# Every product of the macaron block in plain fp32 instead of three fp32r parts

## The reference

```python
def _L0_ffn_ref(x, ...):
    shared = silu(x @ shared_gate.T) * (x @ shared_up.T) @ shared_down.T
    probs = sigmoid(x @ router_w.T + routing_bias)          # 8 experts
    scores, indices = top_k(probs, 2); scores /= sum(scores)
    g = silu(einsum('th,ehi->tei', xf, gate_w)); u = einsum('th,ehi->tei', xf, up_w)
    return shared + einsum('tei,eih,te->th', g * u, down_w, w)   # inner size 256
def _L0_attn_ref(x, ...):   # 16 heads of 8, linear attention over 256 tokens
    phi_q, phi_k = silu(q * s) + 1, silu(k * s) + 1
    return ((phi_q @ (phi_k.T @ v)) @ Wo.T + bo)
x = x + 0.5 * ffn(layernorm(x)); x = x + attn(layernorm(x)); x = x + 0.5 * ffn(layernorm(x))
```

## Time and profile before

| what | value |
|---|---|
| median of 3 runs | 795.73 us (795.63 to 799.72) |
| profiled execution | 798.22 us, of it 796.5 us span |
| PE busy | 682.1 us (86%) |
| DVE busy | 571.3 us (72%) |
| POOL busy | 533.0 us (67%) |
| ACT busy | 471.7 us (59%) |
| mean granted clock of TensorE | 0.921 |

### The profile page before, as it was taken

How to read it: one execution, slowest core, us unless ns; L and a number is a source line. 1 busy time by engine, 2 the same in 40 slices (tenths; PEclk the granted TensorE clock), 3 DMA queues, 4 the chain that set the end, 5 groups by cost and what they waited for, 6 DMA issues and landing times. The chain is left out here.

```text
span 796.5 us, 17786 instructions
## 1 busy us (share of the span) xinstructions
PE 682.1 (86%) x5133; PEld 639.2 (80%) x5133; DVE 571.3 (72%) x1886; ACT 471.7 (59%) x866; POOL 533.0 (67%) x564
## 2 busy tenths in 40 slices
PE   7574979772799999999789889999778999999990
PEld 6464869662799999999678788888677999999990
DVE  7778787771355787877688988899875555777672
ACT  5353453331467777786657666866425677777760
POOL 1457777777777777776166666777774577777672
PEclk9778788987899999999799999999979999999995
DMA  9312221141544555552122111111333535666545
GB/s 278 123 52 77 81 64 55 55 145 54 156 132 125 157 170 166 156 156 58 51 62 67 41 38 45 45 44 51 86 105 83 146 104 149 208 207 200 184 144 168
DMA packets 63337, 89.40 MB, mean 112 GB/s; under 512 B 13194, under 2 KB 43788, under 8 KB 63244
## 3 DMA queue, kind: packets, MB, share of 16 engines
q1 hardware_dynamic: 46348, 53.37, 23.4%
q0 software_dynamic: 16896, 34.90, 13.1%
HBM read 46.10 MB, written 42.12 MB: 111 GB/s over the span
## 5 line engine op out<-in xcount | busy, mean ns | idle before, releaser
L608 POOL DMA_INDIRECT x_rows<-send,send_to x256 | 248.5, 971 | 135.9 <-issue 71.6
L620 POOL DMA_INDIRECT y_rows<-send,y_to x272 | 264.2, 971 | 100.7 <-issue 73.7
L1637 DVE TENSOR_TENSOR h<-silu_g,u_bank 128x512 f32<-128x512 f32 x136 | 93.5, 687 | 114.3 <-ACT silu_g L758 107.8
L733 ACT ACTIVATE slot_gu<-w_gu 128x1024 fp32r x130 | 137.8, 1060 | 36.8 <-issue 36.7
L1013 PE MATMUL y_bank<-w_dn,h 128*128 x1088 | 143.7, 275 | 0.1
L1013 PEld LDWEIGHTS y_bank<-w_dn,h 128*128 128x128 f32 x1088 | 133.2, 192 | 0.3 <-issue 0.3
L855 PE MATMUL g_bank<-xT_hi,slot_gu 128*128 128x256 f32 x260 | 85.8, 330 | 9.9 <-DVE xT_lo L1628 9.2
L928 PEld LDWEIGHTS y_bank<-w_dn,h 128*128 128x128 f32 x512 | 69.2, 212 | 23.3 <-issue 20.6
L928 PE MATMUL y_bank<-w_dn,h 128*128 128x128 f32 x512 | 70.1, 296 | 19.0 <-DVE x L1234 19.0
L758 ACT ACTIVATE silu_g<-g_bank 128x512 f32<-128x512 f32 x136 | 78.8, 579 | 12.0 <-PE g_bank L857 11.5
L677 ACT ACTIVATE send<-x,shift,rstd 128x128 f32<-128x128 f32 x128 | 52.6, 482 | 37.7 <-DVE shift L1196 26.1
(11 more groups left out here) (270 smaller groups left out, 1626.0 us busy)
## 6 DMA issues: line engine op xcount, KB each, us to landing
send<-x_rows SPq DMA_DIRECT2D x130, 130.0 KB
y_pair<-y_rows SPq DMA_DIRECT2D x32, 512.0 KB
y_rows<-send,y_to POOLq DMA_INDIRECT x272
x<-x_in SPq DMA_DIRECT2D x16, 256.0 KB, 7.3
x_rows<-send,send_to POOLq DMA_INDIRECT x256
out<-x SPq DMA_DIRECT2D x16, 256.0 KB
w_raw<-w_experts SPq DMA_DIRECT2D x15, 256.0 KB, 3.1
x_rows<-pad SPq DMA_DIRECT2D x16, 130.0 KB, 2.4
```

The lines of the kernel that those rows point to most:

```text
L608: pool.indirect_dma_start(x_rows, bass.IndirectOffsetOnAxis(ap=send_to[b % SEND_TO_RING][:, w, k:k + 1], axis=0), send[ring_of(f, t)][:, w ...
L620: pool.indirect_dma_start(y_rows, bass.IndirectOffsetOnAxis(ap=y_to[k][:, j:j + 1], axis=0), y_out[f][k][:, j, :], None).then_inc(y_sent[k ...
L733: act.activation(slot_gu[n % 2][:].rearrange("p a n -> p (a n)"), w_gu[:, bass.ds(e, 1)].rearrange("p e a n -> p (e a n)").bitcast(F32), A ...
L1637: dve.tensor_tensor(h[par][0][:], silu_g[par][:], u_bank[par][:], ALU.mult).then_inc(slot_h_done, 1)
```

## The change

All high and low parts are gone, and each product is one plain fp32 matmul.

- `three`, `split_high`, `split_low`, `low`, `slot_low` and the router's split are removed. `gate_up`, `slot_gate_up`, `project`, `query` and `router` issue one matmul where there were three (router: two).
- The shared expert's weights are loaded straight to `w_gu`, those of the eight others by one DMA behind x. The loads through `w_raw` and their waits go.
- ACT's copy of a slot's weights is 512 columns instead of 1024. In a mixed slot ACT copies two experts' weights from `w_gu`, and `load_mixed_weights` and `mixed_gate_up` go.
- `route` has 25 steps instead of 26. `phi_k` and `v_sb` get buffers of their own.

```diff
+            sp.dma_start(w_gu[:, 0, :], w_experts[0, :, 0:2 * INNER]).then_inc(shared_loaded, 16)
...
+            sp.dma_start(w_gu[:, 1:, :], w_experts[1:, :, 0:2 * INNER].rearrange("e p n -> p e n")).then_inc(experts_loaded, 16)
...
-            for e in range(1, EXPERTS):
-                wait_count(sp, split_lo, 0 if e == 1 else split_expert(e - 2))
-                sp.dma_start(w_raw[e % 2][:], w_experts[e, :, 0:2 * INNER]).then_inc(w_loaded[e % 2], 16)
...
-                i = entry(s)
-                e = act.value_load(w_table[0:1, i:i + 1], min_val=1, max_val=ROUTED)
-                wait_count(act, slot_u_psum, n - 1)
-                act.activation(slot_gu[n % 2][:].rearrange("p a n -> p (a n)"),
-                               w_gu[:, bass.ds(e, 1)].rearrange("p e a n -> p (e a n)").bitcast(F32),
-                               ACT.Copy).then_inc(slot_gu_done, 1)
...
+                for j, i in enumerate(half_entries(s) if mixed(n) else (entry(s),)):
+                    e = act.value_load(w_table[0:1, i:i + 1], min_val=1, max_val=ROUTED)
+                    if j == 0:
+                        wait_count(act, slot_u_psum, n - 1)
+                    last = act.activation(slot_w[j][n % 2][:], w_gu[:, bass.ds(e, 1)].rearrange("p e n -> p (e n)"), ACT.Copy)
+                last.then_inc(slot_w_done, 1)
...
-                three(g_bank[k][:], (w[:, 0, g], w[:, 1, g]), xs)
-                three(u_bank[k][:], (w[:, 0, u], w[:, 1, u]), xs).then_inc(gu_psum, 1)
+                pe.matmul(g_bank[k][:], w[:, g], xT[par][:], start=True, stop=True)
+                pe.matmul(u_bank[k][:], w[:, u], xT[par][:], start=True, stop=True).then_inc(gu_psum, 1)
...
-                    pe.matmul(logits, xT_hi[t % XT_RING][:, s], router_parts[:], start=True, stop=False)
-                    last = pe.matmul(logits, xT_lo[t % XT_RING][:, s], router_parts[:], start=False, stop=True)
+                    last = pe.matmul(route_bank[:, (i + j) * ROUTED:(i + j + 1) * ROUTED], xT[t % XT_RING][:, s], router_w[:],
+                                     start=True, stop=True)
...
-                        last = three(bank_[:, c * ROWS:(c + 1) * ROWS], (w[:, 0, i], w[:, 1, i]), xs)
...
+                            last = pe.matmul(bank_[:, k:k + width],
+                                             w[par][:, base + c * P:base + (c + 1) * P],
+                                             xT[par][:, j * width:(j + 1) * width], start=True, stop=True)
...
-                dve.tensor_tensor(xT_lo[n % 2][:, 0:ROWS], slot_tr[n % 2][:, 0:ROWS],
-                                  xT_hi[n % 2][:, 0:ROWS].bitcast(F32), ALU.subtract).then_inc(slot_lo_done, 1)
```

More of the change, by code:

```diff
@@ L80 @@
 FIRST_STEPS, TABLE_STEPS = 19, 60
-TABLE_PIECES = {"last tile": (1, 8), "dispatched": (8, 22), "low": (22, 29), 0: (29, 35), 1: (35, 41)}
+TABLE_PIECES = {"last tile": (1, 8), "dispatched": (8, 22), "first slot": (22, 29), 0: (29, 35), 1: (35, 41)}
 TWO_BANKS_FROM = 2 * TILES - 2
@@ L134, in macaron @@
         x = sb("x", [P, tiles, TT])
-        w_raw = two("w_raw", [P, 2 * INNER])
-        w_gu = sb("w_gu", [P, EXPERTS, 2, 2 * INNER], F32R)
+        w_gu = sb("w_gu", [P, EXPERTS, 2 * INNER])
+        slot_w = [two(f"slot_w{j}_", [P, 2 * INNER]) for j in range(JS)]
         w_dn = sb("w_dn", [P, EXPERTS, HALVES, P])
[L139 to L146, removed]
+        w_attn_sb = sb("w_attn_sb", [P, 4 * P])
+        wo = w_attn_sb[:, 3 * P:4 * P]
+        router_w = sb("router_w", [P, ROUTED])
         bias_b = sb("bias_b", [P, ROUTED])
@@ L184, in macaron @@
         xn = two("xn", [P, SUB, P])
[L185 to L188, removed]
+        xT = ring(XT_RING, "xT", [P, TT])
+        attn_xT = two("attn_xT", [P, TT])
         send = ring(SEND_RING, "send", [P, PICKS, SUB, ROW])
@@ L381, in mixed @@
             return n % slots in MIXED_AT
[L383 to L387, removed]
         def entry(s):
@@ L1584, in dispatch @@
                     route(f, b, 0, MASK_STEP)
-                    if ahead:
-                        low((FFN, f, ahead[0]))
                     multiply_tile(f, ts[0])
@@ L1594, in dispatch @@
                         whole_table(f, 0, 1)
-                    if len(ahead) > 1:
-                        low((FFN, f, ahead[1]))
                     if b + 2 < len(BATCHES[f]) and NORM_OF[(FFN, f, BATCHES[f][b + 2][0])][1] == 0:
@@ L1656, in slot_stage @@
                         slot_results(f, s - 2)
-                    if s + 1 < slots:
-                        slot_low(f, s + 1)
                     if s == 0:
-                        table_piece(f, "low")
-                    if f == 0 and s == slots - 1:
-                        low((ATTN, 1, 0))
+                        table_piece(f, "first slot")
                     slot_multiply(f, s)
@@ L1682, in slot_stage @@
                 if f == 0:
-                    low((ATTN, 1, 1))
                     value(0, 0)
@@ L1751, in middle @@
                         mask_heads(i)
-                    if 0 <= i < tiles - 2:
-                        low((ATTN, 1, i + 2))
                     if 0 < i + 1 < tiles:
```

247 lines of the change are left out of this document (74 added, 173 removed).

## The result

The changed kernel takes 814.59 us (median of 4 runs, 812.58 to 815.06), the kernel before, run beside it, 797.3 (795.63 to 799.72). The ratio is 1.021, with a 95% interval of 1.017 to 1.025. Slower, as forecast, and inside the range, but by 17 us, where the forecast's own terms came to 35. The profiled execution took 814.64 us, 812.9 of it span.

The account below looks back on a forecast made before the run. PE was taken to bound the slot stages, POOL even with it, and DVE the attention turns. Terms 17.6 + 16.1 + 2 - 1 = +34.7 us on 798.2 gave 832.9, as median 830.4, forecast 830; range 811 to 846.

Parts of the forecast that it names:

- The price of a plain product: On PE, a plain record of 256 columns takes 0.217 us; a product takes 0.435 us against 0.352 for three fp32r parts.
- The first rival: On PE, wide plain records stream as fast as fp32r, a slot's products take 0.94 us; 774 us, chance 0.05.
- The slot stages: PE-bound full slots each take 0.34 us longer; +17.6 us in stage one, +16.1 us in stage two.
- POOL's stalls and its tail: Slower PE removes 2.5 us of full-ring stalls in stage one and 3.3 us behind stage two's last slots.
- The attention turns: PE takes over from DVE as bound, 12.8 us a turn over 15 turns; +2 us, bounds -18 and +16.
- Start and dispatch: Ahead of 55.25 us, DVE loses 4.6 us at most, longer products cost 2.5 to 5; -1 us, between -3 and +2.
- The eight slots ahead wait for rows and tables: Stage two's slots before slot 8 wait for rows and tables; no time change was counted for them.
- SP loses the loads of the mixed weights ... hidden: In SP's queue, the mixed slots' weight loads go away; claimed hidden, with no gain counted.
- nothing comes of it: In the slots, ACT's fewer copies and DVE's lost low part bring no gain, as both have a quarter of the stage free.
- The second rival: The attention turns give back all that DVE loses, -18 us instead of +2; 810 us, chance 0.13.
- the handover: The stretch from the last attention addition to slot 8 of stage two; forecast change 0 us.
- The third: PE-bound attention turns meet waits and low clock, 13.6 us a turn, and slots cost +0.37 us; 848 us, chance 0.17.

## Why the prediction came out as it did, step by step

**The price of a plain product** was right: 0.215 us for a record of 256 columns (0.217 forecast), 2.84 for a slot's period (2.86). The first rival, wide plain records as fast as fp32r, is refuted at its root; its bound was 0.176. That the number could be had from a single 0.21 in the earlier trace rows decided the case.

The Trainium skill (FP8 and Floating Point Precision, TensorE Precision Notes) with its four passes for fp32 stands: 4 x 256 columns at 2.4 GHz are an estimate of 0.427 us a product, and the trace has 0.43.

**The slot stages**: +15.9 and, with the tail, +15.7 us against 17.6 and 16.1. A slot costs 0.32 us more, not 0.34. POOL's stalls and its tail went as predicted: the end takes 3.1 us less (3.3).

**The attention turns**: -6.5 against +2. PE as the bound of the later turns was right, 12.6 us a turn (forecast 12.6 and 0.2 of waits), PE busy 129 of 130 us. That DVE had set them at 12.1 before is not what the trace shows: in turns 9 to 12 PE is busy 11.7 to 11.9 us and DVE 10.9 to 11.1, so PE was the fuller engine already, with a short wait for DVE's low part. The last eight took 94.4 us and take 98.7, +4.3, as the terms say.

The step that failed is the one that set all 15 turns at 12.8. The first seven took 93.9 us before, 13.4 on average, and take 83.2 (9.0 to 13.5). Of these 10.7 us, 8.1 lie in turns 1, 2, 4 and 7, which before ran at a mean clock of 0.77, 0.80, 0.81 and 0.88 and after at 1.00; the forecast had taken off 1.7 us for all 15 turns for the pauses and the clock. DVE's part is shown for the third to the sixth turn: idle work there costs 3.2 us. Why the clock stays full in after isn't known; in two kernels with the same work in the turns it fell again in the first two. So a mean over unlike turns hid a gain, and part of the gain is the clock.

**Start and dispatch**: +2.8 against -1. The forecast set longer products at half clock against DVE's relief and took the relief to win. The head got longer, and PE's products are on its chain: half of those of three tiles taken away brought the third batch forward. What share of the +2.8 is theirs isn't shown, and the +2.8 itself is known to 2 us only: in the seven kernels with the new head on chips like the first, slot 5's silu starts between 206.1 and 207.8, against 205.0.

**"The eight slots ahead wait for rows and tables"** was the larger miss: 12.0 of the 18 us by which the sum was off. The sentence was true and priced at nothing, as if rows and tables came when they came. They come by a chain that the change cut at two places. "SP loses the loads of the mixed weights ... hidden" was wrong: 4.3 us, shown by putting the loads back. And the slot's low part that DVE lost, 0.42 us, went into "nothing comes of it" as work of an engine with room, and not as what PE waits for: 4.8 us, shown by adding the wait, with its two idle subtracts, to after. Both stood in the trace of before, as 4.64 us of PE's idle time and as SP's queue. The sum of both, 9.1, leaves 2.9 of the 12.0, if they add. The kernel with three parts in the full slots alone, with SP's list of after, takes 54.6 us there, 7.7 above after and 4.3 below before; the 7.7 are the wait and 2.9 more, 0.8 of which stay with the first two slots plain (47.7). So most of the 2.9 goes with slots that are short while the table is late; how, wasn't taken apart.

**The second rival** (turns give back all that DVE loses, 810) named the right place and had a share of the truth: the measured 814.6 lies nearer to its 810 than to 830, but the turns gave 6.5 us, not 18, and the handover gave the rest. The third (848) is refuted: the clock stood at half for 89 us of the span, 126 before (from the means of 0.945 and 0.921), and for none of the turns.

**The range** (811 to 846) holds the result 3.6 us above its low end. That is partly luck: it was drawn wide for the turns, no term or rival had the handover's 12 us in it, and the head's miss of 3.8 us went the other way. Right by their mechanism were the side of the result, the price of a product and the slots.

## What to carry to other kernels

Ahead of a removed operation ask not only what it costs on its engine but who waits for it and what stands in front of it in its list: here a 0.42 us subtract queued behind table steps held the next engine for 4.6 us. A stretch between two stages is to be followed as a chain, queue by queue, and never set to zero because "it waits for something else". And where a change helps in one stage and costs in another, take it only where it helps: three parts in the full slots from the third on, and plain products in the first two of each stage and in everything outside the full slots, gave 788.9 us, below both kernels.

## What was not expected of the hardware

On two of the four chips of the experiments the kernel before takes 1,003 and 1,017 us instead of 797. The trace shows no longer operation: scatters take 0.97 us, records of 256 columns 0.215. But several engines stop together: between slots 5 and 67 of stage one ACT and DVE are both idle for 1.5 to 3.5 us ten to fifteen times in each of the six traces from these chips, 21 to 35 us in all, and not once in the eight others. The kernel with PE's wait on the second slow chip, SP's queue, then ACT and DVE in the same stretch:

```profile
287.82 2.89 SPq L456 DMA_DIRECT2D send<-x_rows  x2
```

```profile
293.62 0.60 ACT L695 ACTIVATE silu_g<-g_bank 128x512 f32<-128x512 f32 x1 [3.02 <-PE g_bank L911]
```

```profile
294.24 0.69 DVE L1512 TENSOR_TENSOR h<-silu_g,u_bank 128x512 f32<-128x512 f32 x1 [5.59 <-ACT silu_g L695]
```

```profile
295.07 1.15 PE L927 MATMUL y_bank<-w_dn,h 128*128 x8 [2.10 <-DVE h L1512]
...
296.32 1.92 PE L911 MATMUL g_bank<-xT,slot_w 128*128 128x256 f32 x4
```

ACT stands idle for 3 us before a silu whose bank PE has ready, and SP takes 2.89 us for two row loads that took 1.44 in after. Then PE goes on at half clock. What holds the engines isn't in the trace. Slots 5 to 67 of stage one take 218 to 223 us there, with plain and with three-part products alike, and after with PE's wait added, 1.027 of the kernel before on the other chip, takes 0.981 and 0.983 of it in its single runs there. After itself wasn't run on them, nor was the kernel before profiled on them, so that the sign of the change turns is likely and not shown. A verdict of 2% on this kernel holds for chips of the kind it was taken on.

The second thing is what went with one wait. In three kernels PE stood without work for 4.64, 4.79 and 4.85 us at the handover and went on at half clock: the sixteen down records that follow take 3.61, 3.39 and 2.82 us, against 1.95 in after, where the wait isn't there. Here, a wait of PE cost more than its length.
